# Attention keys of the second layer, turned two tiles at a time on TensorE instead of one

## What is computed

```
kv_r   = rope(ctx_512)                                    # (8, 1444, 64): keys before W_kr, and values
q_r    = einsum(rope(einsum(hidden_q @ Wq.T, w_kc_q)), W_qr)
k_r    = einsum('bld,hdr->bhlr', kv_r, W_kr)
scores = einsum('bhsr,bhlr->bhsl', q_r, k_r)
ctx_c  = einsum('bhsl,bld->bhsd', softmax(scores), kv_r)
out    = x + (per head: ctx_c @ w_kc_kv, then @ Wo.T)     # then the feed-forward
```

## Time and profile before

| | |
|---|---|
| median of 3 runs | 866.11 us (864.6 to 867.09) |
| the profiled execution | 860.95 us |
| its span, first to last instruction | 859.2 us |
| PE busy | 801.9 us, 93% of the span |
| DVE busy | 577.7 us, 67% |
| POOL busy | 453.7 us, 53% |
| ACT busy | 381.0 us, 44% |
| turns of the keys, L1106 | 96, of 0.265 us each |
| copies of the keys, kh and khl | 48, of 0.55 to 0.57 us each |
| low_keys, L1887 | 24, of 0.65 us each |

### The profile page before, as it was taken

The page is one execution under the profiler, slowest core; times in us unless marked ns, Lnnn a source line. Parts: engine busy times, 40 slices in busy tenths (PEclk is TensorE's granted clock), DMA queues, the critical chain, the costliest instruction groups (busy, mean ns, idle before and its releaser), DMA issues.

```text
span 859.2 us, 15505 instructions
## 1 busy us (share of the span) xinstructions
PE 801.9 (93%) x5850; PEld 592.6 (69%) x5850; DVE 577.7 (67%) x1118; ACT 381.0 (44%) x853; POOL 453.7 (53%) x466
## 2 busy tenths in 40 slices
PE   8888799999987999999999999999999999999986
PEld 6666567999765677676776677666776767766545
DVE  4688543223586756778787877878778777786545
ACT  3588511222302545444544544544454364445441
POOL 3000138000411877778767767786776766567640
PEclk9999979999999999999999999999999999999998
DMA  8731245997101001000000000000010000000000
GB/s 304 247 127 51 70 158 199 319 324 269 52 7 37 1 3 28 11 1 29 11 2 11 23 11 11 24 11 1 11 33 2 10 8 11 1 15 11 8 9 10
DMA packets 21897, 53.04 MB, mean 62 GB/s; under 512 B 7482, under 2 KB 15940, under 8 KB 19392
## 3 DMA queue, kind: packets, MB, share of 16 engines
q1 hardware_dynamic: 20800, 50.42, 17.4%
q0 software_dynamic: 1024, 1.64, 0.6%
HBM read 45.80 MB, written 5.36 MB: 60 GB/s over the span
## 4 chain that ended last, share of the span: by engine, by line
PE 69%; DVE 13%; ACT 7%; issue 5%; DMA 3%; POOL 1%; SPq 0%; POOLq 0%; ACTq 0%; DVEq 0%
PE ps L1145 15%; PE ps L1157 12%; PE ps L1125 7%; PE ps L1063 6%; PE ps L1007 4%; PE ps L1182 3%; PE ps L1068 3%; PE ps L1091 3%; ACT sm L1415 3%; PE ps L1020 2%; DMA xs<-xs_scratch 2%; DVE nm L1897 2%; DVE xyz L1868 2%; PE ps L856 1%; DVE xyz L1864 1%
## 5 line engine op out<-in xcount | busy, mean ns | idle before, releaser
L612 POOL TENSOR_TENSOR acc<-acc,pt 120x800 f32<-120x800 f32 (+1 forms) x157 | 299.0, 1905 | 90.2 <-ACT pt L1595 57.9
L1595 ACT ACTIVATE pt<-ps 120x400 f32<-120x400 f32 (+1 forms) x384 | 189.9, 505 | 223.8 <-PE ps L1145 213.4
L1897 DVE TENSOR_REDUCE nm<-ps 128x1 f32<-128x482 f32 (+1 forms) x336 | 213.6, 655 | 103.3 <-PE ps L1125 101.3
L1145 PE MATMUL ps<-qh,khl 128*120 128x400 f32 (+1 forms) x384 | 157.5, 410 | 10.2 <-ACT pt L1595 7.1
L1157 PE MATMUL ps<-pt,kv 120*64 120x400 f32 (+1 forms) x768 | 143.9, 510 | 0.0
L1125 PE MATMUL ps<-khl,qh 128*128 128x482 f32 (+1 forms) x336 | 131.1, 391 | 6.1 <-DVE nm L1897 5.2
L1145 PE MATMUL ps<-ql,kh 65*120 65x400 f32 (+1 forms) x384 | 133.5, 348 | 0.0
L1145 PEld LDWEIGHTS ps<-qh,khl 128*120 128x120 f32 (+1 forms) x384 | 70.4, 183 | 57.3 <-issue 32.2
L1157 PEld LDWEIGHTS ps<-pt,kv 120*64 120x64 f32 (+1 forms) x768 | 50.4, 137 | 64.2 <-issue 55.1
L634 POOL TENSOR_TENSOR rstd<-veps,mhalf 100x1 f32<-100x1 f32 (+2 forms) x21 | 14.0, 668 | 127.0 <-DVE veps L1728 84.5
L1145 PEld LDWEIGHTS ps<-ql,kh 65*120 65x120 f32 (+1 forms) x384 | 70.7, 184 | 5.0
(11 more groups left out here) (255 smaller groups left out, 1182.9 us busy)
## 6 DMA issues: line engine op xcount, KB each, us to landing
ew<-in_expert_w_dram SPq DMA_DIRECT2D x14, 1536.0 KB, 7.7
fw<-in_ternary_w_dram SPq DMA_DIRECT2D x6, 512.0 KB, 8.4
spread<-inv_scratch SPq DMA_DIRECT2D x30, 100.0 KB, 2.7
craw<-in_ctx_dram SPq DMA_DIRECT2D x8, 360.0 KB
woT<-in_wo_t_dram SPq DMA_DIRECT2D x1, 2048.0 KB, 14.8
xs_scratch<-zero SPq DMA_DIRECT2D x1, 1792.0 KB, 8.8
xs<-xs_scratch SPq DMA_DIRECT2D x14, 128.0 KB, 6.7
ys_scratch<-ysb SPq DMA_DIRECT2D x14, 128.0 KB, 7.0
```

The lines of the kernel that those rows point to most:

```text
L612: nc.gpsimd.tensor_tensor(total[r, :, :], before[r, :, :], pt[j % PT_BUF][r, :, :], ALU.add).then_inc(p_added, 1)
L1145: last = mm(ps[0:key_rows(t), k % 2, 0:HT], lhs[:, keys], rhs[:, HT * a:HT * a + HT], start=first, stop=not first)
L1595: nc.scalar.activation(pt[j % PT_BUF][0:rows, k % 2, :], ps[0:rows, k % 2, 0:HT], ACT.Exp).then_inc(p_ready, 1)
L1897: nc.vector.tensor_reduce(nm3[0:w, i, n:n + 1], ps[0:w, 3 + m % 2, 0:MN], AX.X, ALU.max).then_inc(m_reduced, 1)
```

## The change

One transpose takes two neighbouring tiles, 128 columns: the even tile's 64 numbers land on partitions 0 to 63 of bank 5, the odd tile's on partitions 64 to 127. A group is two transposes into 2n columns instead of four into 4n (n is 121 or 120). The destinations stay as they were, with tile behind tile. So a copy takes one parity e: it reads the half of the partitions that has it (turned_keys) and writes every other run of n columns (every_other). ACT makes four copies of 64 x 2n instead of two of 64 x 4n, DVE two subtractions of 64 x 2n instead of one of 64 x 4n. For the odd tiles the subtraction takes the high part from khl on partitions 64 to 127 and not from kh1, so that both of its inputs lie on the same partitions. Semaphores and slots are unchanged; each is raised by the last instruction of its step.

```diff
+        def turned_keys(j, e):
+
+            n = key_rows(4 * j)
+            return ps[CD * e:CD * e + CD, 5, 0:2 * n].rearrange("p (i k) -> p i k", i=2)
+
+        def every_other(keys, j, e):
+
+            k0, n = key_start(4 * j), key_rows(4 * j)
+            return keys[:, k0:k0 + 4 * n].rearrange("p (i e k) -> p i e k", e=2, k=n)[:, :, e, :]
...
-                for t in range(4 * j, 4 * j + 4):
-                    at = key_start(t) - key_start(4 * j)
-                    last = turn(ps[0:CD, 5, at:at + key_rows(t)], kv[b % KV_BUF][0:key_rows(t), t, :],
-                                ident[0:key_rows(t), 0:key_rows(t)])
+                n = key_rows(4 * j)
+                for i in range(2):
+                    t = 4 * j + 2 * i
+                    last = turn(ps[:, 5, n * i:n * i + n], kv[b % KV_BUF][0:n, t:t + 2, :].rearrange("p t d -> p (t d)"),
+                                ident[0:n, 0:n])
                 last.then_inc(k_turned, 1)
...
-                k0 = key_start(4 * j)
-                n = key_start(4 * j + 4) - k0
-                keep(kh1[b % 2][0:CD, k0:k0 + n], ps[0:CD, 5, 0:n])
-                keep(khl[b % 2][CD:128, k0:k0 + n], ps[0:CD, 5, 0:n]).then_inc(k_hi, 1)
+                for e in range(2):
+                    keep(every_other(kh1[b % 2][0:CD, :], j, e), turned_keys(j, e))
+                    last = keep(every_other(khl[b % 2][CD:128, :], j, e), turned_keys(j, e))
+                last.then_inc(k_hi, 1)
...
-                k0 = key_start(4 * j)
-                n = key_start(4 * j + 4) - k0
-                tt(khl[b % 2][0:CD, k0:k0 + n], ps[0:CD, 5, 0:n], kh1[b % 2][0:CD, k0:k0 + n].bitcast(F32), ALU.subtract)\
-                    .then_inc(k_kept, 1)
+                for e in range(2):
+                    high = (kh1[b % 2][0:CD, :], khl[b % 2][CD:128, :])[e].bitcast(F32)
+                    last = tt(every_other(khl[b % 2][0:CD, :], j, e), turned_keys(j, e), every_other(high, j, e), ALU.subtract)
+                last.then_inc(k_kept, 1)
```

## The result

| | before | after |
|---|---|---|
| median, runs of one session | 866.6 us (864.6 to 868.73) | 883.08 us (882.37 to 884.49) |
| ratio, 95% interval | | 1.0195 [1.0166, 1.0224] |
| the profiled execution | 860.95 us | 882.46 us |
| its span, mean granted clock | 859.2 us, 0.987 | 880.7 us, 0.981 |

The kernel is 2.0% slower. I had forecast slower by 5.4 us; it is 16.5 by the medians, and 883.1 lies outside the range of 865 to 875. The profiled execution of before stood 5.6 us under its median, that of after 0.6, so the two traces differ by 21.5.

What follows compares the result with a forecast made beforehand. Bound: PE's chain, with turns, copies, low_keys and rope in series in places. Loop +3.9 us and batch 0 ahead of it +1.5 us make +5.4 us, put on the median 866.11: 871.5 us, range 865.0 to 875.0.

Steps and rivals of the forecast that it cites:

- Turns: PE, all 24 groups: two wide turns in place of four, each about 0.103 us, -0.20 us per group.
- Copies: ACT, key copies: four of 0.38 us without overlap in place of two, 1.55 against 1.13, +0.42 us per group.
- Subtractions: DVE, low_keys: two of 0.41 us in place of one, +0.28 us until the next DVE instruction.
- Third group: Layer-2 loop, b = 0 to 6: rope and ct (b = 0: a max chunk) +0.50 us later, all on the chain.
- Second: Second group in the loop: low_keys runs behind other DVE work, so only PE's gain counts, -0.20 us.
- First: First group in the loop: +0.50 us uses up 0.23 of room before q_big, leaving +0.27; for b = 0, +0.2.
- Per period: One batch's loop period: 0.27 - 0.20 + 0.50 = 0.57 us six times, 0.5 once, +3.9 us in all.
- Batch 0 up to turn_x3: Ahead of the loop, batch 0's three groups in series until norm_x3: together +1.5 us.
- the rivals about overlap: ACT's copies and DVE's subtractions overlap: 863.2 us, faster, chance 0.11; only the copies overlap: 865.0 us, no change, chance 0.15.
- a second group on the chain: Loop: the second group loses its cover, seven times another +0.2 to +0.5 us; part of a rival with chance 0.10.
- Slower: Whole kernel: the outcome of a slower kernel, chance 0.74, against 0.15 within about 0.3% and 0.11 faster.
- The one on the far side: Rival: second group comes onto the chain, or a wide turn costs double in all 24 groups; 874 to 876 us, chance 0.10.

Runs made afterwards that it cites:

- the turns alone: Kernel before with two wide turns per group in place of four, copies and subtraction unchanged, half of the keys left out: 0.9949, 863.65 us.
- the wait of POOL: Changed kernel with one wait added, so that POOL's sum of weights in slot 17 starts only when ct is made: 1.0109 to the kernel before, 875.01 us.
- With the collision and batch 0's part taken out: Changed kernel with POOL's slot-17 sum waiting for ct and batch 0's groups in the old form: 1.0073 to the kernel before, 873.61 us.
- the two fillers: Kernel before with one or two short DVE reductions behind the third group's low_keys, b = 1 to 6: one 1.003, 868.96 us; two 1.0196, 883.95 us.
- two slot numbers: LOW_KEY_SLOT (6, 12, 15) to (8, 12, 16), against the kernel before: changed kernel 0.991, old kernel 0.9922, changed with batch 0 in old form 0.9865.

## Why the prediction was wrong

**Right, step by step.**
- *Turns*: 48 of 0.27 us, 0.105 to 0.107 apart, -0.20 per group; the turns alone give -0.6 per period.
- *Copies*: 96 of 0.36 to 0.37 with 0.012 between them. Four take 1.49 against 1.13, +0.36 where I took +0.42. They don't overlap; the rows on the key copies had told more than the Trainium skill, page "ScalarE: Activation LUTs", section "What ACT_TABLE_LOAD costs", whose overlap of 93 ns appears between none of them.
- *Subtractions*: 0.40 and 0.41, 0.013 apart, and the rope starts 0.03 behind the second (437.67 + 0.41, 438.11). +0.28, as given.
- *Third group without the collision* (with the wait of POOL): turns to output projection 6.66 us against 6.22, +0.44 where I gave +0.50. *Second*: -0.20. *First*: +0.46 where I gave +0.27. Its room of 0.23 went as forecast and PE starts 0.05 behind the rope. But the rope's end moved by 0.57 against the turns and not by 0.50, and PE then takes 1.58 us from q_big's start to the next turns where it took 1.47.
- *Per period* +0.70 where I summed 0.57. *Batch 0 up to turn_x3* +1.36 where I gave +1.5.

So the local sum was right to 0.13 per period, partly because two terms erred in opposite directions, and the rivals about overlap fall with the rows that I had weighed against them. With the collision and batch 0's part taken out, the kernel is 6.3 us slower than before, 2.7 either way, and the forecast for the loop alone was 3.9. Two slips in the working change nothing in this: 0.86 less 0.57 is 0.29 and not 0.28, and a second group on the chain would cost 0.4 to 0.7 more per period (from -0.20 to +0.2 or +0.5), which is what gives the 874 to 876 of that rival.

**The step that failed**: "rope and ct (a max chunk for b = 0) come +0.50 later relative to the turns, all of it on the chain", together with "POOL, the DMAs and the semaphores are as before". I moved ct by 0.50 and kept its duration. POOL did nothing new, but a DVE instruction that both engines' timelines put 0.22 us ahead of one of POOL's was moved past it, and it then took 1.88 instead of 0.58: +1.3 us, six times, 7.8 us. The place to see it was there: the chain had ct as its last link before PE, and POOL's timeline of the same stretch, which I did not read, showed a sum starting during ct that took 2.09 where others take 1.89. The wait of POOL and the two fillers show this cause from both sides.

**The second one**: "The added pauses of PE are under a microsecond each, and I cost the clock at nothing." PE's pauses before the output projection grew by 1.95 us each (0.85 to 2.80), and in one period of the profiled execution half clock came with it (+2.7 us). One stretch of it came behind the 1.16 ahead of turn_x3, and a second 31 us later, still before the first score (+3.1 in all). Together 5.8 us of the traces' 21.5. This part is not the same in every execution. By the medians, 16.5 - 7.8 (collision) - 4.2 (local, six periods) - 0.7 (b = 0) - 1.4 (ahead of the loop) leaves 2.4 us for it and for the tail. The first of these stretches goes with the pause ahead of turn_x3 in every profile: in the four kernels with 1.16 us it came within 2.6 us behind turn_x3's start, and in the nine with 0.50 or 0.51 it did not. The four are also those with batch 0 in the new form, and no run tells the pause from the form. In the loop half clock is more frequent with a longer pause (the counts are at the end), but five of the six pauses of 2.80 in after had none, and what decides there stays open.

Slower, to which I gave 0.74, came out, but what I had summed makes up 6.3 of the 16.5 us (4.2 + 0.7 + 1.4). So the direction was right for the reason given only in that part. None of the rivals was what happened. The one on the far side had the second group on the chain or a wide turn at double cost; that group kept its -0.20 and a wide turn costs 0.106.

## What to carry to other kernels

When an edit shifts an instruction of DVE that reads two tensors in SBUF, lay POOL's timeline beside DVE's and ask which of the two starts first before and after. Here a shift of 0.37 us cost 1.9, about the whole of POOL's instruction, and nothing in the page's sums shows it but a mean duration that has grown in a line which no one edited. And before an instruction-saving edit is written off, move its consumers off the chain: here two slot numbers turn 2.0% slower into 0.9% faster, and 1.3% with batch 0 left as it was, while they give the old kernel 0.8% without the edit.

## What the runs showed of the hardware

- **DVE and POOL exclude each other** on these operations for nearly an instruction's whole length. ct (two inputs in SBUF, 128x400) takes 0.58 alone or first, 1.88 if it starts 0.41 behind POOL's 120x800 sum, 2.10 if 0.21, 2.15 if 0.15 behind, 2.29 if with it, each time ending 0.42 to 0.43 after the sum. The other way round the sum grows from 1.89 to 2.09 and 2.28. The Trainium skill, page "SBUF — State Buffer", section "Who interferes with whom", says that DVE's second pair of ports is GpSimd's as well and goes by an exclusive lock, and that a DVE instruction with both inputs in SBUF contends with one of GpSimd that reads SBUF. The trace agrees in both directions. The rope's products of L1879 read PSUM and SBUF; four of them took 1.49 us beside POOL's rotation of the keys and the start of its sum, as long as in the kernel before.
- **The granted clock** fell to half, for 3.4 or 6.8 us at a time in the places looked at here, with some pauses of PE and not with others of the same length. Over the profiles of all 13 kernels, for PE's pause ahead of the output projection in the periods b = 1 to 6, such a stretch began within the pause or in the microsecond behind it in 10 of 19 cases with a pause of 2.75 to 2.81 us, in 3 of 18 with 1.49 to 1.59, in none of 23 with 0.84 to 1.03, and in none of the 18 without a pause. A period with such a stretch was 1.4 to 3.0 us longer.
- **A wide turn costs as much as a narrow one**: two transposes of two tiles, 128 columns wide, start 0.105 to 0.107 us apart and those of one tile, 64 wide, 0.103, both with 120 or 121 moving columns.
